# A fused image and text layer on one core: eight transfers of the rows of maxima, and another order within a turn

## The chip, the cores and the metric

One core of a Trainium2 chip runs the whole program. Its engines are TensorE (PE, matmuls and transposes), VectorE (DVE), ScalarE (ACT), GpSimd (POOL) and SyncE (SP, which issues most of the transfers). The metric is the device time of one execution in microseconds; lower is better.

## What is computed

The reference takes 32 images of 224 x 224 and 32 texts of 77 tokens. It embeds 196 patches per image with one matmul, adds positions, appends the texts (274 tokens of 192 numbers), and runs one layer: causal attention with 12 heads, then a two-sided mixture of experts with capacity.

```python
h = _L0_tok_ref(x, ...)                       # patches @ W.T + b, class token, positions
h = jnp.concatenate([h, txt], axis=1)         # (32, 274, 192)
h = h + _L0_attn_ref(_layernorm(h), ...)
h = h + _L0_ffn_ref(_layernorm(h), ...)

def _L0_attn_ref(X, Wq, bq, Wk, bk, Wv, bv, Wo, bo):
    q = rope(X @ Wq + bq)
    k = rope(X @ Wk + bk)
    v = X @ Wv + bv
    scores = jnp.einsum('bqhd,bkhd->bhqk', qh, kh) / jnp.sqrt(jnp.float32(hd))
    weights = jax.nn.softmax(jnp.where(causal, scores, -jnp.inf), axis=-1)
    out = jnp.einsum('bhqk,bkhd->bqhd', weights, vh).reshape(B, S, D)
    return out @ Wo + bo
```

## The kernel before

The program has two phases. The first, in the function `attention`, embeds, attends and routes, image by image; it fills about the first 1,000 us. The second, `experts`, runs the expert matmuls. The change touches the first alone.

**Tiling.** An image's 274 tokens are two tiles of 128 and a tail of 18. The tails of four images share one tile (`xnt`, `Vt`, `UsbT` and so on), so their work comes once in four images. The 12 heads are three groups (j = 0, 1, 2) of four.

**Turns.** Every engine runs the same loop, `for t in map(Turn, range(TURNS))`. In a turn five images are worked on at once, each in a later stage: `t.new` is embedded (E0 and E1, its two token tiles, lines 525, 1236 and 1252), `t.pre` is turned (X: transposes of its normed tokens `xn`, line 534), projected (V0, V1, QK0, QK1, lines 541 and 542), rotated on DVE (lines 1103, 1104) and its heads turned (KQ0 to KQ2, line 574); `t.mid` gets the maxima of its scores; `t.at` gets its scores and weights; `t.fin` its values (PV1, PV2), their transposes (UT0, UT1), division, AT and the output projection WO (lines 549, 550). `t.end` is added up and stored. Where an item is none, its lines are left out. The tails' steps (`t.tail[k]`: XTt, QKt, Vt, KQt0, KQt1, UTt, ATt, WOt) stand in one turn out of four each.

**Maxima and scores.** The softmax needs each query's maximum before its exponentials. Scores are computed twice. Round M*j* (`maxs`, line 587) writes the scores of a head group with queries on the partitions; `reduce_max` on DVE masks them into `capped` (line 1037) and reduces them along the keys into `nm` (lines 1039, 1041; the banks are free after the instruction of line 1039). A further round T (`maxs_tail`, lines 597 and 601) does this for the 18 tail queries, reduced at line 1299. PE transposes `nm` (MT, line 737), ACT rounds it into `mT[:, 0]` (line 852), DVE puts what is left over into `mT[:, 1]` (line 1325), and SP carries the rows of `mT` as further rows into `HX`, the operand of the score matmuls (lines 476, 477). In the next turn, round S*j* (`scores`, line 616) computes the scores again with keys on the partitions and the maximum taken off by these rows; ACT takes the exponential (`weights`, line 778), GpSimd masks (lines 911, 912), and PE multiplies with the values (PV*j*, `values`, line 628).

**Banks.** All rounds M, S and T share one set of four PSUM banks, `round_banks`, in the order M0, S0, M1, S1, M2, T, S2 of the table ROUNDS. A round starts when the one before it has been read (`fill_round`). All other results of PE (E0, X, V0 and so on) go to four further banks in turn, in the order of the table STEADY: each use waits until the use four places before it has been emptied, and the two tables must name the uses in the order in which PE's code issues them.

**Queues.** Every engine runs its instructions in the order in which the code issues them, and SP its transfers too. What can stall it is a semaphore. At the round S0 PE waits for all transfers of the rows of maxima:

```python
if j == 0:
    pe.wait_ge(mrow_in[b % 2], 224 * (b // 2 + 1))
```

PE's order in a turn before is: PV1, M0 (after a wait for KQ0, KQ1 and KQ2), PV2, E0, S0, X, E1, M1, V0, QK0, S1, UT0, UT1, QK1, (KQt), M2, V1, PV0, (XTt, ATt, UTt), T, AT, (RK, QKt), KQ0, KQ1, MT, S2, (Vt), KQ2, WO, (WOt).

## Time and profile before

| | us |
|---|---|
| median of 3 runs | 1520.82 |
| lowest and highest of them | 1489.72, 1523.75 |
| the profiled execution | 1509.2 |
| its span, first to last instruction | 1507.4 |
| mean granted TensorE clock over the span | 0.888 of full |
| PE busy | 1216.2 (81%) |
| DVE busy | 965.3 (64%) |
| ACT busy | 561.2 (37%) |
| POOL busy | 664.4 (44%) |

The rows below come from one profiled execution. A timeline row is start, duration, engine, line, operation, output<-inputs, and in brackets how long the engine had been idle and which instruction released it by the profile; neighbouring instructions of one kind are merged (x12). The brackets name what came last by the profile, not always the semaphore that held. SPq rows are issues of transfers. Overlapping instructions count once in busy times. Granted clock 1.00 is TensorE at 2.4 GHz, 0.5 at 1.2 GHz.

### The profile page before, as it was taken

The page shows a single profiled execution, that of the slowest core. Times are in us where ns is not written, and L with a number is a line of the kernel's source. Part 1 is how long each engine was busy: PE and PEld are TensorE (multiplying, and loading weights), DVE is VectorE, ACT ScalarE, POOL GpSimd, SP SyncE. Part 2 cuts the span into 40 slices and gives each one's busy share as a digit, 9 for nine tenths or more (in the row PEclk, how much of TensorE's full clock was granted, in tenths as well). Part 3 has the DMA queues.
Part 4 walks back from the last instruction along what each step waited for, and adds up shares of the span by engine and source line. Part 5 has one row for each costly group of instructions (what it writes and reads, how often), then busy time and mean ns, then how long its engine had stood idle before and what let it go on. Part 6 is the DMA issues. An engine that isn't in the chain of part 4 may idle for free.

```text
span 1507.4 us, 33177 instructions
## 1 busy us (share of the span) xinstructions
PE 1216.2 (81%) x12302; PEld 1013.1 (67%) x12302; DVE 965.3 (64%) x2211; ACT 561.2 (37%) x1039; POOL 664.4 (44%) x1097
## 2 busy tenths in 40 slices
PE   6688888888888888888888887763899687889993
PEld 5566666666666666665766665553799587889993
DVE  4657767778777776777778767646697433445441
ACT  1134434433433333333333433222355244445550
POOL 2134334334444543543454443342542665555665
PEclk8689989999999988989999987675899798999997
DMA  6011121113213212311231221138576565667751
GB/s 195 2 37 37 36 67 41 37 50 101 71 49 103 83 49 62 114 58 51 72 109 54 70 91 36 52 96 314 197 242 232 155 209 178 217 202 247 235 190 32
DMA packets 86676, 168.65 MB, mean 112 GB/s; under 512 B 17886, under 2 KB 60005, under 8 KB 86512
## 3 DMA queue, kind: packets, MB, share of 16 engines
q1 hardware_dynamic: 72848, 140.48, 29.3%
q0 software_dynamic: 13664, 26.00, 4.8%
q8 instruction: 101, 1.65, 0.5%
q14 instruction: 63, 0.52, 0.1%
HBM read 124.00 MB, written 45.45 MB: 112 GB/s over the span
## 4 chain that ended last, share of the span: by engine, by line
PE 37%; DVE 28%; issue 14%; SPq 9%; DMA 3%; POOL 3%; another core or an unknown queue 3%; ACT 2%; POOLq 0%; DVEq 0%; ACTq 0%
PE h_ps L1770 9%; PE y_ps L1781 7%; SPq L476 7%; PE gen L525 5%; DVE capped L1037 5%; DVE xn L1070 3%; DVE nm L1039 2%; PE round_banks L616 2%; DMA HX<-mT 2%; DVE ropeB L1104 2%; DVE ropeA L1103 2%; PE gen L534 2%; PE round_banks L601 1%; PE gen L628 1%
## 5 line engine op out<-in xcount | busy, mean ns | idle before, releaser
L778 ACT ACTIVATE PT<-round_banks 128x1752 f32<-128x1752 f32 x96 | 156.7, 1632 | 211.9 <-PE round_banks L616 210.9
L911 POOL TENSOR_SCALAR_AFFINE_SELECT PT<-PT 128x512 f32<-128x512 f32 x192 | 117.8, 638 | 210.8 <-ACT PT L778 210.4
L1860 ACT ACTIVATE Gl<-h_ps,W 128x256 f32<-128x256 f32 x264 | 117.4, 474 | 229.8 <-PE h_ps L1770 152.5
L1781 PE MATMUL y_ps<-W,Gl 128*128 128x192 f32 x1056 | 186.5, 329 | 7.3 <-issue 5.2
L1770 PE MATMUL h_ps<-XH,Wh 128*128 128x256 f32 x528 | 157.0, 312 | 43.0 <-issue 17.4
L1781 PEld LDWEIGHTS y_ps<-W,Gl 128*128 128x128 f32 x1056 | 174.1, 192 | 8.9 <-issue 6.9
L525 PE MATMUL gen<-w_emb,xT 128*128 128x192 f32 (+1 forms) x768 | 166.8, 377 | 7.9 <-DMA ident<-in_ident_dram 7.9
L525 PEld LDWEIGHTS gen<-w_emb,xT 128*128 128x128 f32 (+1 forms) x768 | 136.4, 193 | 22.1 <-DMA ident<-in_ident_dram 7.9
L1770 PE MATMUL h_ps<-XH,Wl 128*128 128x256 f32 x528 | 148.0, 299 | 0.0
L616 PEld LDWEIGHTS round_banks<-HX 18*128 18x128 f32 (+5 forms) x2304 | 79.4, 196 | 95.0 <-DMA HX<-mT 60.8
L1770 PEld LDWEIGHTS h_ps<-XH,Wh 128*128 128x128 f32 x528 | 110.2, 209 | 48.7 <-issue 34.9
L1670 POOL DMA_INDIRECT out_dram<-Y,sid x76 | 82.2, 1082 | 136.8 <-DVE Y L1953 117.6
L1037 DVE TENSOR_TENSOR capped<-round_banks,masks_f 128x1024 f32<-128x1024 f32 x96 | 116.3, 1212 | 37.0 <-PE round_banks L587 37.0
L616 PE MATMUL round_banks<-HX 18*128 18x146 f32 (+9 forms) x2304 | 88.2, 284 | 62.7 <-DMA HX<-mT 54.3
L1929 DVE TENSOR_TENSOR Wl<-W,Wh 128x768 fp32r<-128x768 f32 x88 | 84.2, 958 | 71.9 <-ACT Wh L1840 37.1
L1041 DVE TENSOR_REDUCE nm<-capped 128x8 f32<-128x1024 f32 x96 | 116.0, 1209 | 0.0
L1770 PEld LDWEIGHTS h_ps<-XH,Wl 128*128 128x128 f32 x528 | 110.3, 209 | 0.0
L1045 DVE SCALAR_TENSOR_TENSOR HX<-HX,slots,gen 128x512 fp32r<-128x512 f32 x96 | 70.0, 746 | 62.4 <-ACT HX L792 54.1
L628 PE MATMUL gen<-PT,V 128*17 128x274 f32 (+1 forms) x1536 | 97.1, 376 | 0.8 <-POOL PT L912 0.8
L920 POOL TENSOR_TENSOR rr<-ropeA,ropeB 128x384 f32<-128x384 f32 x64 | 65.9, 1030 | 70.5 <-DVE ropeB L1104 70.4
L541 PE MATMUL gen<-w_qkv,xnT 97*128 97x200 f32 (+1 forms) x256 | 92.7, 444 | 0.0
L587 PEld LDWEIGHTS round_banks<-HX 32*128 32x128 f32 (+1 forms) x1536 | 58.2, 203 | 50.8 <-issue 34.2
(276 smaller groups left out, 2508.3 us busy)
## 6 DMA issues: line engine op xcount, KB each, us to landing
W<-in_experts_dram SPq DMA_DIRECT2D x44, 771.0 KB
W<-in_experts_dram SPq DMA_DIRECT2D x44, 672.0 KB
xT<-in_xT_dram SPq DMA_DIRECT2D x32, 591.0 KB, 5.2
X<-sorted_d SPq DMA_DIRECT2D x35, 386.0 KB
stage<-rows_d SPq DMA_DIRECT2D x64, 192.0 KB
HX<-mT SPq DMA_DIRECT2D x384, 2.0 KB
rows_d<-h SPq DMA_DIRECT2D x32, 192.0 KB
out_dram<-h SPq DMA_DIRECT2D x32, 192.0 KB
```

The lines of the kernel that those rows point to most:

```text
L476: sp.dma_start(q[:, j, tok(k)], m[12 * j + 2 * k:12 * j + 12:3, :]).then_inc(mrow_in[b % 2], 16)
L525: mm = pe.matmul(g[0:m, 0:D], xT[b % 2][:, c, cols], w_emb[:, c, :], start=(c == 0), stop=(c == EC - 1))
L541: pe.matmul(o, xTs[:, 0, tok(k)], w[0:KC + 1, 0, cols], start=True, stop=False)
L616: mm = pe.matmul(R[0:m, i, at:at + n], x[rows, JG + j, klo:klo + m], q[rows, j, qlo:qlo + n], start=first, stop=not first, skip_group_chec ...
L628: mm = pe.matmul(g[SLOT * i:SLOT * i + HD + 1, lo:S], v, pt[:, i, at:at + n], start=(k == 0), stop=(k == 2), tile_position=(0, SLOT * i), ...
L778: act.activation(PT[(JG * b + j) % 2][:], R[:, :, 0:438], ACT.Exp, scale=SCALE).then_inc(exps, 1)
L911: pool.affine_select(x[:, :, at:at + P], x[:, :, at:at + P], [[0, GH], [1, P]], ALU.is_ge, 0.0, base=0, channel_multiplier=-1)
L1037: dve.tensor_tensor(capped[:], blocks[:, :, 0:3:2, :], masks[:].rearrange("p (a b k) -> p a b k", a=1, b=1).broadcast_to([P, GH, 2, P]), A ...
L1041: dve.tensor_reduce(x[:, :, 0:3:2], capped[:], AX.X, ALU.max, negate=True).then_inc(capped_read, 1)
L1770: mm = pe.matmul(h_ps[f % 3][:, 0:ROWS], w[t.par][:, cols], x, start=(k == 0), stop=(k == len(products) - 1))
L1781: mm = pe.matmul(y_ps[t.par][:, k * D:(k + 1) * D], Gl[t.par][:, f, k * P:(k + 1) * P], W[t.i][:, W2O + f * D:W2O + (f + 1) * D], start=(f ...
L1860: act.activation(Gl[t.par][:, f, :], h_ps[f % 3][:, 0:ROWS], ACT.Gelu, bias=W[t.i][:, B1O + f:B1O + f + 1]).then_inc(g_ready, 1)
```

## The change

Three things are changed, all within a turn.

1. **Rows of maxima.** `nm` has its columns by head (12) and tail (4) for each of the two token tiles, and the middle block's maxima go to a tile of their own, `nm1`. PE transposes it in two pieces to 16 rows of 256. A head group is then four neighbouring rows, and SP carries it with one transfer for each of the two parts of `mT`: eight transfers in all, the four of group 0 and of the tails first. Each head group has its own semaphore, and S*j* waits for its own rows.
2. **PE's order.** M0 comes first in the turn and no longer waits for KQ2 (M1 does). Then PV1, PV2, X, S0, E0, M1, V0, V1, QK0, S1, UT0, UT1, QK1, (KQt), M2, E1, (XTt, ATt, UTt), T, PV0, AT and on as before. The turned tokens X come ahead of S0, the first round with weights, and E1 ahead of T.
3. **The others follow.** On ACT the copy of X comes ahead of the exponential of S0, V1's copies behind V0's, and PV0's behind the tails' copies. On DVE E0's addition and first statistic stand just ahead of the second reduction, E1's addition, statistic and both aggregations behind the third, and the scaling of `xn` behind the remainder `mT`. On GpSimd the root for it stands behind the tail copy.

```diff
-STEADY = [("PV1", 4), ("PV2", 4), ("E0", 0), ("X", 1), ("E1", 0), ("V0", 1), ("QK0", 1), ("UT0", 4), ("UT1", 4), ("QK1", 1),
-          ("KQt0", "1"), ("KQt1", "1"), ("V1", 1), ("PV0", 3), ("XTt", "0"), ("ATt", "8"), ("UTt", "7"),
+STEADY = [("PV1", 4), ("PV2", 4), ("X", 1), ("E0", 0), ("V0", 1), ("V1", 1), ("QK0", 1), ("UT0", 4), ("UT1", 4), ("QK1", 1),
+          ("KQt0", "1"), ("KQt1", "1"), ("E1", 0), ("XTt", "0"), ("ATt", "8"), ("UTt", "7"), ("PV0", 3),
...
-        nm = sb("nm", [P, P])
-        mT = sb("mT", [P, 2, P], F32R)
+        nm = sb("nm", [P, 2, HEADS + GH])
+        nm1 = sb("nm1", [P, HEADS])
+        mT = sb("mT", [HEADS + GH, 2, 2 * P], F32R)
...
-                        for j in range(JG):
-                            for k in range(2):
-                                sp.dma_start(q[:, j, tok(k)], m[12 * j + 2 * k:12 * j + 12:3, :]).then_inc(mrow_in[b % 2], 16)
+                        sp.dma_start(q[:, 0, 0:2 * P], m[0:GH, :]).then_inc(mrow_in[0][b % 2], 16)
                         sp.dma_start(q[:, 0:JG, 2 * P:S],
-                                     m[36:40, 0:JG * SLOT].rearrange("i (j r) -> i j r", r=SLOT)[:, :, 0:TL]).then_inc(mrow_in[b % 2], 16)
+                                     m[HEADS:, 0:JG * SLOT].rearrange("i (j r) -> i j r", r=SLOT)[:, :, 0:TL]).then_inc(mrow_in[0][b % 2], 16)
+                    for j in range(1, JG):
+                        for w in range(2):
+                            q, m = HX[b % 3][HD + w:P:SLOT, 1].bitcast(F32), mT[:, w, :].bitcast(F32)
+                            sp.dma_start(q[:, j, 0:2 * P], m[GH * j:GH * j + GH, :]).then_inc(mrow_in[j][b % 2], 16)
...
-                if j == 0:
-                    pe.wait_ge(mrow_in[b % 2], 224 * (b // 2 + 1))
+                pe.wait_ge(mrow_in[j][b % 2], (64 if j == 0 else 32) * (b // 2 + 1))
...
+                if t.mid is not None:
+                    have("KQ0", t.mid)
+                    have("KQ1", t.mid)
+                    maxs(t.mid, 0)
                 if t.fin is not None:
                     values(t.fin, 1)
-                if t.mid is not None:
-                    for c in range(3):
-                        have(f"KQ{c}", t.mid)
-                    maxs(t.mid, 0)
...
-                    filled("MT", t.mid, pe.transpose(g[:, 0:P], nm[:], ident[:]))
+                    for k in range(2):
+                        mm = pe.transpose(g[0:HEADS + GH, tok(k)], nm[:, k, :], ident[:])
+                    filled("MT", t.mid, mm)
...
-                    act.activation(mT[:, 0, :], g[:, 0:P], ACT.Copy).then_inc(m_rounded, 1)
+                    act.activation(mT[:, 0, :], g[0:HEADS + GH, 0:2 * P], ACT.Copy).then_inc(m_rounded, 1)
```

The moved pieces read best as the engines' orders. First PE, a turn of kind B from the end of WO to the first rows of the projections (L587 is a round M, L616 a round S, L628 PV, L525 with 128 rows E0 and with 69 rows E1, L534 X), before:

```order
L587 MATMUL round_banks<-HX 128x256 x8
L587 MATMUL round_banks<-HX 128x128 x8
L628 MATMUL gen<-PT,V 17x274 x4
L628 MATMUL gen<-PT,V 17x146 x4
L628 MATMUL gen<-PT,Vt_2 17x18 x4
L525 MATMUL gen<-w_emb,xT 128x192 x6
L616 MATMUL round_banks<-HX 128x274 x8
L616 MATMUL round_banks<-HX 128x146 x8
L616 MATMUL round_banks<-HX 128x18 x8
L534 MATMUL gen<-ident,xn 96x128 x4
L525 MATMUL gen<-w_emb,xT 69x192 x6
L587 MATMUL round_banks<-HX 128x256 x8
```

and now, from the second of the two PV of that place on (every line number is higher by 2 or 3):

```order
L630 MATMUL gen<-PT,V 17x274 x4
L630 MATMUL gen<-PT,V 17x146 x4
L630 MATMUL gen<-PT,Vt_2 17x18 x4
L537 MATMUL gen<-ident,xn 96x128 x4
L618 MATMUL round_banks<-HX 128x274 x8
L618 MATMUL round_banks<-HX 128x146 x8
L618 MATMUL round_banks<-HX 128x18 x8
L528 MATMUL gen<-w_emb,xT 128x192 x6
L590 MATMUL round_banks<-HX 128x256 x8
L590 MATMUL round_banks<-HX 128x128 x8
```

X has moved from behind S0 to ahead of it, E0 from ahead to behind, and E1 is gone from between S0 and the next round M. The same rounds' places on DVE, from the last reduction of the turn, before (L1299 reduces T, L1325 is the remainder `mT`, the first L1103 and L1104 rotate QKt, which only kind A has):

```order
L1041 TENSOR_REDUCE nm<-capped 128x4x2
L1299 TENSOR_REDUCE nm<-round_banks 96x4
L1304 TENSOR_TENSOR nm<-nm 128x12
L1045 SCALAR_TENSOR_TENSOR HX<-HX,slots,gen 128x2x256 x2
L1325 TENSOR_TENSOR mT<-gen,mT 128x128
L1103 TENSOR_TENSOR ropeAt<-gen,cosw 128x384
L1104 TENSOR_TENSOR ropeBt<-gen,sinw 128x384
L1045 SCALAR_TENSOR_TENSOR HX<-HX,slots,gen 128x2x256
```

and now:

```order
L1046 TENSOR_REDUCE nm<-capped 128x4x2
L1280 TENSOR_TENSOR h<-gen,base 69x192
L1066 BN_STATS stat<-h 128x6
L1071 BN_AGGR mv<-stat 128x2 x2
L1296 TENSOR_REDUCE nm<-round_banks 96x4
L1300 TENSOR_TENSOR nm<-nm 128x12
L1050 SCALAR_TENSOR_TENSOR HX<-HX,slots,gen 128x2x256 x2
L1321 TENSOR_TENSOR mT<-gen,mT 16x256
L1075 TENSOR_SCALAR xn<-h,mv,rstd 128x192 x2
L1108 TENSOR_TENSOR ropeAt<-gen,cosw 128x384
L1109 TENSOR_TENSOR ropeBt<-gen,sinw 128x384
L1050 SCALAR_TENSOR_TENSOR HX<-HX,slots,gen 128x2x256
```

E1's addition, statistic and aggregations stand between the third reduction and that of T, and the scaling of `xn` between the remainder and the rotation of QKt. SP's transfers of a turn, before and now:

```order
L476 DMA HX<-mT 4x128 x6
L477 DMA HX<-mT 4x3x18
L476 DMA HX<-mT 4x128 x6
L477 DMA HX<-mT 4x3x18
L392 DMA xT<-in_xT_dram 128x1182
```

```order
L475 DMA HX<-mT 4x256
L476 DMA HX<-mT 4x3x18
L475 DMA HX<-mT 4x256
L476 DMA HX<-mT 4x3x18
L481 DMA HX<-mT 4x256 x4
L393 DMA xT<-in_xT_dram 128x1182
```

Fourteen issues became eight, and the four that S0 waits for are the first.

## Rows read from the trace of the kernel before

**Rows 1.** Busy time by stretch (length, engines, PEclk, DMA share, GB/s): turns, then many

```profile
238.80:269.90 31.10, 26.87 (x312) 21.42 (x310) 23.13 (x51) 13.39 (x28) 12.22 (x24) 0.89 0.16 48
269.90:296.50 26.60, 21.59 (x295) 16.60 (x295) 20.22 (x42) 9.93 (x17) 9.94 (x20) 1.00 0.17 51
296.50:323.90 27.40, 21.90 (x299) 16.75 (x299) 21.08 (x46) 10.97 (x21) 9.93 (x20) 1.00 0.16 48
323.90:354.00 30.10, 26.70 (x307) 19.89 (x308) 24.11 (x62) 10.08 (x18) 10.93 (x23) 0.89 0.21 63
...
528.00:558.20 30.20, 24.91 (x299) 18.91 (x299) 21.05 (x46) 10.97 (x21) 13.41 (x25) 0.89 0.19 60
...
238.80:916.60 677.80, 568.42 (x6949) 436.13 (x6947) 509.63 (x1153) 256.22 (x464) 299.97 (x574) 0.92 0.23 70
```

**Rows 2.** Groups by line, PE: busy, mean ns | idle before, by releaser

```profile
L616 PE MATMUL round_banks<-HX 18*128 18x146 f32 (+9 forms) x2304 | 88.2, 284 | 62.7 <-DMA HX<-mT 54.3 <-DVE nm L1039 6.4 <-ACT PT L778 1.7
```

**Rows 3.** Timeline of kind B, first part: start, us, engine, line, tiles [idle before]

```profile
271.32 0.28 DVE L1325 TENSOR_TENSOR mT<-gen,mT 128x128 fp32r<-128x128 f32 x1
...
271.64 3.25 SPq L476 DMA_DIRECT2D HX<-mT  x6
...
273.47 0.75 DVE L1045 SCALAR_TENSOR_TENSOR HX<-HX,slots,gen 128x512 fp32r<-128x512 f32 x1 [1.86 <-ACT HX L792]
...
274.47 0.69 PE L587 MATMUL round_banks<-HX 32*128 32x256 f32 x16 [0.63 <-ACT Usb L782]
...
275.20 1.23 DVE L1037 TENSOR_TENSOR capped<-round_banks,masks_f 128x1024 f32<-128x1024 f32 x1 [0.44 <-PE round_banks L587]
...
275.97 2.22 PE L525 MATMUL gen<-w_emb,xT 128*128 128x192 f32 x12
...
276.35 0.68 DVE L1039 TENSOR_REDUCE nm<-round_banks 128x4 f32<-128x512 f32 x1
...
278.83 0.57 SPq L477 DMA_DIRECT2D HX<-mT  x1
...
280.44 0.66 DVE L1070 TENSOR_SCALAR xn<-h,mv,rstd 128x192 f32<-128x192 f32 x2
...
280.49 0.88 PE L616 MATMUL round_banks<-HX 32*128 32x274 f32 x24 [2.31 <-DMA HX<-mT]
...
281.42 1.63 ACT L778 ACTIVATE PT<-round_banks 128x1752 f32<-128x1752 f32 x1 [4.89 <-PE round_banks L616]
```

**Rows 4.** Timeline of the same turn, second part

```profile
283.93 0.35 DVE L1252 TENSOR_TENSOR h<-gen,base 69x192 f32<-69x192 f32 x1 [2.83 <-PE gen L525]
...
284.20 0.60 DVE L1061 BATCH_NORM_STATS2 stat<-h 128x6 f32<-128x192 f32 x2
...
285.01 1.19 DVE L1037 TENSOR_TENSOR capped<-round_banks,masks_f 128x1024 f32<-128x1024 f32 x1
...
288.77 1.35 DVE L1070 TENSOR_SCALAR xn<-h,mv,rstd 128x192 f32<-128x192 f32 x2
...
288.93 1.07 POOL L920 TENSOR_TENSOR rr<-ropeA,ropeB 128x384 f32<-128x384 f32 x1 [2.40 <-DVE ropeB L1104]
...
292.03 1.22 DVE L1037 TENSOR_TENSOR capped<-round_banks,masks_f 128x1024 f32<-128x1024 f32 x1
...
293.99 0.32 PE L597 MATMUL round_banks<-tmask,identb 128*96 128x18 bf16 x4 [1.78 <-DVE nm L1039]
...
295.09 1.30 DVE L1299 TENSOR_REDUCE nm<-round_banks 96x4 f32<-96x1096 f32 x1
...
296.52 0.33 PE L737 MATMUL gen<-ident,nm 128*128 128x128 f32 x1
```

**Rows 5.** Timeline of kind A, the projection of the tails' values (Vt)

```profile
241.98 1.04 PE L541 MATMUL gen<-w_qkv,xntT 97*128 97x200 f32 x2 [2.10 <-DVE ropeBt L1104]
```

**Rows 6.** Timeline, S0 of the last two turns

```profile
929.31 1.39 PE L616 MATMUL round_banks<-HX 32*128 32x274 f32 x24 [4.03 <-DMA HX<-mT]
...
962.92 1.49 PE L616 MATMUL round_banks<-HX 32*128 32x274 f32 x24 [4.91 <-DMA HX<-mT]
```

More of the change, by code:

```diff
@@ L349, in attention @@
         nmax_ready = sem("nmax_ready")
-        mrow_in = sems("mrow_in", 2)
+        mrow_in = [sems(f"mrow{j}_in", 2) for j in range(JG)]
         exps, masked = sem("exps"), sem("masked")
@@ L669, in _ @@
                     turn_tokens("X", t.pre, xn, 2)
+                if t.at is not None:
+                    scores(t.at, 0)
                 if t.new is not None:
-                    embed(t.new, 1)
+                    embed(t.new, 0)
                 if t.mid is not None:
+                    have("KQ2", t.mid)
                     maxs(t.mid, 1)
@@ L965, in _ @@
                     pool.tensor_copy(HX[b % 3][:, :, :, 2 * P:S], HXt[:, :, :, b % 4, :].bitcast(F32)).then_inc(tails_copied, 1)
+                if t.new is not None:
+                    root(LN1, t.new, 2)
+                    root_std(t.new)
                 if t.tail[0] is not None:
```

94 lines of the change are left out of this document (44 added, 50 removed).

## The prediction

> **What bounds the kernel now.** I first cut the span into turns by their TensorE (PE) transposes of `nm`, and put the busy times of the turns side by side [rows 1]. A turn has one image in each of five stages, and four kinds of turn repeat, since the tails of four images share a tile. I call them A (from 238.8 us), B (269.9), C (296.5) and D (323.9). In B, PE is busy 21.6 of 26.6 us and VectorE (DVE) 20.2, so neither fills it: the turn is a chain between them through the one set of round banks. The reader should see there that PE computes a round of scores, DVE or ScalarE reads it, and only then can PE write the next. Next came the groups by line, for what PE waits for: 54.3 us before the first score round S0, for the rows of maxima that SP copies into `HX` [rows 2]. The timeline of B shows both halves of it. `mT` is ready at 271.6, 14 transfers follow at 0.54 each, the last is issued at 278.83, and S0 starts at 280.49, 1.66 us after that issue; PE stood for 2.31 us [rows 3]. Everything behind S0 is late with it: ScalarE's exp (1.63), then E1, then DVE, which stands 2.83 us until E1 is there, and only then the second max reduction at 285.01 [rows 3, 4].
>
> **The change, part by part.** I take B from `mT` ready to the next `nm` transpose.
>
> *Rows of maxima.* S0 now waits for four transfers, not fourteen: 0.54 + 0.57 + 0.54 + 0.57 = 2.2 us of issue, the last beginning at 271.6 + 1.65 = 273.3; plus 1.66 they are there at 275.0, where they were at 280.4. A row transfer is now twice as long (4 rows of 256 numbers). The trace has no such transfer; below, it costs what one of 128 costs (0.54), above, as much as the two it replaces (1.08), which puts the landing at 276.1. I take the first. The four for j = 1 and 2 begin before 276 and are wanted 6 us later at the earliest. PE makes two transposes of `nm` for one (0.3 us more), ScalarE and DVE copy 256 columns for 128 (0.28 each now [rows 3]; at most twice that, 0.3 more each).
>
> *M0 first, without KQ2.* The 0.63 us before M0 carries the name of a ScalarE copy, but M0 starts right after DVE's `HX` piece of KQ2 ends (273.47 + 0.75 = 274.22) and the code has the wait for KQ2 there [rows 3]. It goes to M1. But DVE has KQ2's piece and two additions ahead of the reduction anyway: its 0.44 us of idleness before 275.20 say that it was done at 274.8, and there the reduction now begins. The banks are free after the second of its three instructions (1.23 + 0.68), at 276.8. PE has M0, PV1 and PV2 until E0's old start less the 0.63, 275.3, then X (half a us), and waits about 1 us. S0 runs at 276.8 instead of 280.49: 3.7 earlier, and the rows (275.0) leave 1.8 to spare. If that cover is gone, each us of later landing costs one.
>
> *E0 after S0, E1 behind M2.* exp ends at 276.8 + 0.93 + 1.63 = 279.4, E0 (2.2) at 279.9, so M1 loses 0.5 to E0. DVE must finish `xn2`, which hangs on GpSimd and not on S0 (280.44 + 0.66 = 281.1), then E0's addition and one statistic (0.65): the second reduction starts at 281.8 instead of 285.01, 3.2 earlier. From there to the third reduction it took 7.0 [rows 4]; of these, 1.35 was scaling `xn`, which goes behind `mT`: 5.75, so the third is at 287.5 instead of 292.03, 4.5 earlier. E1 on PE fills the 1.78 us in which PE stood before the tail round T. What pays is DVE: its block for E1 took 285.01 - 283.93 = 1.1, of which one statistic (half of 0.60) has gone ahead with E0; 0.8 now stands between the third reduction and that of T, where nothing hides it. The next `nm` transpose is thus 4.5 - 0.8 = 3.7 earlier, at 292.8. PE's own side: T starts 1.96 behind the third reduction, at 289.5; from T to that transpose it took 2.53, and PV0 comes on top (0.9, as PV2 between M0's end at 275.16 and E0 at 275.97): 292.9, just as late. For hops between engines and for this tightness I take off 1.0: **B saves 2.7 us, C the same**. GpSimd's root for `xn` moves behind its tail copy; behind it stand the tail addition and the last causal mask, which come later than it anyway: nothing.
>
> *`xn` behind `mT`.* Its two instructions take 1.35 us where GpSimd's addition of `rr` (1.07) runs beside them, and 0.66 for the same shape (`xn2`) elsewhere [rows 3, 4]. In B and C DVE waits 1.86 us for ScalarE's KQ2 copy just there, which hides it. The Trainium skill (SBUF — State Buffer, Who interferes with whom) says that VectorE and GpSimd share a port pair as an exclusive lock, and the second to come blocks wholly. The two rows agree with it; by the rule the moved pair costs 0.66 where GpSimd is idle and up to a GpSimd instruction more where not.
>
> *Kind A pays.* Its Vt projection waits 2.10 us for DVE's rotation of QKt [rows 5], and `xn` now stands ahead of that rotation: 0.7 to 1.35 more. A has no wait before S0 to win. DVE's later `xn` slot is free, but ScalarE's tail copies end late there, so that gain is mostly lost, and E1's 0.8 comes at the end. Bounds: +0.3 and +2.3; I take **A +1.3**. *Kind D* waited little before S0, but wins the order from M0 to M1 and `xn`'s slot (1.35), and loses 0.8: between 0.5 and 3; I take **-2.0**.
>
> *Sum.* Four turns: -2.7 - 2.7 + 1.3 - 2.0 = -6.1. From the second turn to the last are 30, or 7.5 fours: -46. The last two turns wait 4.03 and 4.91 before S0 [rows 6], more than the 2.3 counted: -5. Then the clock: 238.8 to 916.6 had a mean granted clock of 0.92 [rows 1], that is, stretches at 1.2 of 2.4 GHz that lose up to 0.08 x 678 = 54 us. A and D at 0.89 lose 3.4 each, 39 in the 5.8 fours; 15 are left to B and C, 19 over all 7.5. The same kind C took 27.4 at 1.00 and 30.2 at 0.89. With gaps of about 1 us in place of 2.3 most of that should go: -14. Altogether -65. The profiled execution took 1509.2 (span 1507.4), so 1444; the median of the three runs is 11.6 above it, so **1456 us** there.
>
> **The rivals.**
>
> *Only half is kept.* The gaps move to bank release, E0 delays M1 more than I laid out, or ScalarE's later Usb and `attT` copies hold KQ0. For it: PE and DVE meet within 0.1 us at the end of B in my layout. Against: the second reduction really waited on E1, which waited on S0. B and C save 1.4, D 1, A pays 1.3: -2.5 x 7.5 = -19, ends -5, clock -7: -31, 1490 by the median.
>
> *Nothing is kept.* The rows' wait is hidden slack of a DVE-bound turn and the change moves where PE idles. Against it speak 2.83 us of DVE idleness right behind that wait. About 1515.
>
> *Slower: the end of the turn on DVE.* One mechanism: E1's 0.8 ahead of T's reduction and `xn` (up to 1.35) ahead of the QKt rotation lengthen the path from the third reduction to the next M0 in every turn, while the second reduction does not come earlier. It decides if in B that reduction starts less than 0.8 us earlier than 285.01. Price: 0.8 x 30 = 24, A's rotation 1.35 x 7.5 = 10: +34, 1555.
>
> *The clock stays up.* Gaps of 1 us may leave PE at 2.4 GHz in D too and shorten A's stretch: of the 54 us, 45 come back instead of 14. -46 - 5 - 45 = -96, 1425. Against: A's gap grows to about 3 us and D's behind S2 stays. The Trainium skill (TensorE: Matmul & The Clock Gate, HAM oscillation — how this bites in real kernels) has PE fall to half clock after an idle stretch and stay there until it has been busy a while. The trace agrees only in part: B took a 2.31 us gap at clock 1.00.
>
> **How the numbers follow.** Forecast 0.60 (1436 to 1478 around 1456); half kept 0.16; nothing kept 0.08; slower 0.06; clock stays up 0.10. The range 1425 to 1495 holds the forecast, most of the half and of the clock case, about 8 in 10; the three runs of before spread by 34 us, which this must also cover. A measurement here tells about 2% (30 us) from no change, so faster means below 1490: all of the forecast and of the clock case, and half of the half case, 0.78. Within 2%: the other half and nothing kept, 0.16. Slower: 0.06.
>
> **What would show it.** In the profile after: no idle time before S0 put down to `HX<-mT` beyond a few us in total; S0 about 4 us after M0 in B, with DVE's release before it; DVE no longer idle at E1's addition; PE idle before T under 1 us; A turns longer than 31 us with over 2.5 us before Vt; B and C near 24 us at clock 1.0. I would be wrong if B's second reduction keeps its distance of 9.8 us from the first, if the rows land after 276.8, or if the share of low clock rises.

## The result, and the profile after

| us | before | after |
|---|---|---|
| median of four runs | 1512.12 | 1411.69 |
| lowest and highest | 1489.72, 1523.75 | 1405.82, 1436.51 |
| ratio, with its 95% interval | | 0.9398 [0.9269, 0.9528] |
| the profiled execution, its span | 1509.2, 1507.4 | 1415.52, 1413.7 |
| mean granted clock over the span | 0.888 | 0.911 |
| the 28 turns A to D, seven times | 827.8 | 748.4 |
| granted clock in these | 0.91 | 0.95 |

The change makes the kernel 6.0% faster by the ratio. (The quotient of the two medians is 0.934, inside the interval of the ratio.) An execution now and then comes out some per cent slower than the others of its kernel, whatever the kernel, and the ratios are formed without these. The direction and the main mechanism were forecast; the size was not. The profiled execution is 93.7 us shorter, the forecast was 65, and the median lies below the range that I gave.

First the turns again, by stretch (length, busy time of PE, PE's weight loads, DVE, ACT and POOL, granted clock, DMA share and GB/s), in the kernel after: B, C, D and A as in [rows 1], a later D and A, and the 28 turns.

```profile
245.00:268.30 23.30, 21.41 (x296) 16.53 (x296) 20.39 (x42) 10.00 (x17) 9.64 (x20) 1.00 0.20 58
268.30:293.00 24.70, 21.66 (x301) 16.80 (x301) 21.78 (x48) 10.83 (x19) 10.03 (x21) 1.00 0.18 54
293.00:320.60 27.60, 23.33 (x310) 17.99 (x308) 24.54 (x62) 10.80 (x19) 11.01 (x23) 1.00 0.24 69
320.60:349.60 29.00, 25.04 (x312) 20.11 (x310) 23.20 (x55) 13.60 (x28) 15.96 (x29) 0.94 0.29 92
...
398.20:428.10 29.90, 26.43 (x311) 20.87 (x309) 25.06 (x62) 10.84 (x19) 11.08 (x23) 0.89 0.22 64
428.10:460.10 32.00, 28.05 (x312) 22.03 (x309) 23.44 (x55) 13.54 (x28) 15.81 (x29) 0.84 0.26 83
...
107.60:856.00 748.40, 657.02 (x8456) 511.65 (x8455) 625.93 (x1378) 316.03 (x559) 350.85 (x676) 0.95 0.24 73
```

The same 28 turns of the kernel before:

```profile
122.70:950.50 827.80, 693.16 (x8427) 530.50 (x8425) 613.28 (x1371) 310.34 (x559) 351.18 (x676) 0.91 0.22 66
```

B and C now run at full clock each time, and are 3.3 and 2.7 shorter than the B and C of [rows 1], which had clock 1.00 as well. D ran at 0.89 in [rows 1]; here one D has 1.00 and another 0.89. A is on average as long as it was, 29 to 32, and its length goes with its granted clock.

Then the groups that waited. PE before the rounds S and DVE before the reduction, after (busy, mean ns | idle before them, by releaser; before in [rows 2]):

```profile
L618 PE MATMUL round_banks<-HX 18*128 18x146 f32 (+9 forms) x2304 | 83.8, 273 | 48.5 <-DVE nm L1044 44.4 <-DMA HX<-mT 1.9 <-ACT PT L782 1.8
L600 PE MATMUL round_banks<-tmask,identb 128*96 128x18 bf16 x128 | 10.3, 189 | 12.3 <-DVE nm L1044 12.2
```

```profile
L1042 DVE TENSOR_TENSOR capped<-round_banks,masks_f 128x1024 f32<-128x1024 f32 x96 | 116.7, 1215 | 5.7 <-PE round_banks L590 5.7
```

The wait for the transfers fell from 54.3 to 1.9 over the whole phase. A shorter one for DVE's release of the banks stands there, 48.5 in all before 96 rounds. DVE hardly waits for a round M any more, 5.7 us in 96 reductions where it was 37.0.

The timeline of the first B (start, us, engine, line, tiles, and in brackets the idle time before and its releaser), to be laid beside [rows 3, 4]:

```profile
246.37 0.41 DVE L1321 TENSOR_TENSOR mT<-gen,mT 16x256 fp32r<-16x256 f32 x1
246.81 0.53 SPq L475 DMA_DIRECT2D HX<-mT  x1
...
248.10 0.69 PE L590 MATMUL round_banks<-HX 32*128 32x256 f32 x16
248.57 0.57 SPq L476 DMA_DIRECT2D HX<-mT  x1
249.19 2.15 SPq L481 DMA_DIRECT2D HX<-mT  x4
249.88 1.22 DVE L1042 TENSOR_TENSOR capped<-round_banks,masks_f 128x1024 f32<-128x1024 f32 x1
251.84 0.88 PE L618 MATMUL round_banks<-HX 32*128 32x274 f32 x24 [0.84 <-DVE nm L1044]
...
254.70 1.23 POOL L915 TENSOR_SCALAR_AFFINE_SELECT PT<-PT 128x512 f32<-128x512 f32 x2
254.83 1.11 DVE L1093 SCALAR_TENSOR_TENSOR by_token<-by_token,rstd,w_r 128x8 f32<-128x8 f32 x2 [1.20 <-issue]
...
257.11 1.21 DVE L1042 TENSOR_TENSOR capped<-round_banks,masks_f 128x1024 f32<-128x1024 f32 x1
262.59 2.17 PE L528 MATMUL gen<-w_emb,xT 128*69 128x192 f32 x12
263.09 1.22 DVE L1042 TENSOR_TENSOR capped<-round_banks,masks_f 128x1024 f32<-128x1024 f32 x1
265.05 0.32 PE L600 MATMUL round_banks<-tmask,identb 128*96 128x18 bf16 x4 [0.29 <-DVE nm L1044]
265.94 0.34 DVE L1280 TENSOR_TENSOR h<-gen,base 69x192 f32<-69x192 f32 x1
266.95 1.26 DVE L1296 TENSOR_REDUCE nm<-round_banks 96x4 f32<-96x1096 f32 x1
268.34 0.39 PE L740 MATMUL gen<-ident,nm 128*16 128x128 f32 x2
```

The reader should see the chain in its new order. A transfer of 256 costs 0.53, the row that was not in the trace of before. S0 starts 3.74 after M0, released by DVE; it was 6.02 (280.49 - 274.47 in [rows 3]). From the first to the second reduction it is 7.23 where it was 9.81, and E1 (262.59) fills the stretch ahead of T, where PE now stands for 0.29.

### The profile page after: what moved, and what is told of

Its sections match the earlier page's. It is cut to its first block and busy times, and to the rows that moved or that the text cites. A ratio compares the mean times of both kernels' runs of the same rounds, so it can differ in the third digit from the quotient of the medians.

```text
span 1413.7 us, 33145 instructions
## 1 busy us (share of the span) xinstructions
PE 1169.9 (83%) x12334; PEld 986.8 (70%) x12334; DVE 974.2 (69%) x2211; ACT 567.6 (40%) x1039; POOL 662.6 (47%) x1097
## 5 line engine op out<-in xcount | busy, mean ns | idle before, releaser
L528 PE MATMUL gen<-w_emb,xT 128*128 128x192 f32 (+1 forms) x768 | 150.9, 350 | 8.1 <-DMA ident<-in_ident_dram 8.1
L1774 PEld LDWEIGHTS h_ps<-XH,Wh 128*128 128x128 f32 x528 | 109.0, 206 | 61.4 <-issue 47.7
L528 PEld LDWEIGHTS gen<-w_emb,xT 128*128 128x128 f32 (+1 forms) x768 | 123.2, 178 | 17.8 <-DMA ident<-in_ident_dram 8.1
L618 PEld LDWEIGHTS round_banks<-HX 18*128 18x128 f32 (+5 forms) x2304 | 76.1, 185 | 79.5 <-issue 75.0
L786 ACT ACTIVATE Usb<-gen 128x274 f32<-128x274 f32 x96 | 38.5, 401 | 219.8 <-PE gen L630 217.2
L618 PE MATMUL round_banks<-HX 18*128 18x146 f32 (+9 forms) x2304 | 83.8, 273 | 48.5 <-DVE nm L1044 44.4
L924 POOL TENSOR_TENSOR rr<-ropeA,ropeB 128x384 f32<-128x384 f32 x64 | 63.8, 997 | 126.9 <-DVE ropeB L1109 126.9
L237 POOL DMA_INDIRECT sorted_d<-stage,pos x72 | 73.5, 1020 | 36.8 <-DMA stage<-rows_d 20.1
```

The lines of the kernel that those rows point to most:

```text
L528: mm = pe.matmul(g[0:m, 0:D], xT[b % 2][:, c, cols], w_emb[:, c, :], start=(c == 0), stop=(c == EC - 1))
L618: mm = pe.matmul(R[0:m, i, at:at + n], x[rows, JG + j, klo:klo + m], q[rows, j, qlo:qlo + n], start=first, stop=not first, skip_group_chec ...
L1774: mm = pe.matmul(h_ps[f % 3][:, 0:ROWS], w[t.par][:, cols], x, start=(k == 0), stop=(k == len(products) - 1))
```

## The experiments

Ratios are to the kernel before, run on the same chip, with their 95% intervals. "28 turns" is that stretch of the profiled execution each time, from the third `nm` transpose to the 31st: 827.8 us at clock 0.91 before, 748.4 at 0.95 after. Edits are shown as diffs against the kernel before or after, as named, with parts left out at "...".

The experiments were run in three groups on three chips. The kernel before had a median of 1490.69 us beside the first group (the parts apart, E1 back, rotation first), 1519.15 beside the second (22 and 20 fillings, M0 back, the choice behind `xn`) and 1510.64 beside the third (9 and 8 fillings, the choice in the next turn, `xn` back). So the 28 turns and the clocks of two kernels, and two ratios from different groups, should be compared with some reserve. A turn at clock 1.00 is a better measure: B took 23.6 to 23.7 us in most turns of all the kernels with B's order as in after, whatever the chip.

### The parts apart: the transfers alone, the order alone

Transfers alone is the kernel before with `nm`, `nm1`, `mT`, the eight transfers and a semaphore for each group; no engine's order changes but for these.

```diff
# against before
-                        for j in range(JG):
-                            for k in range(2):
-                                sp.dma_start(q[:, j, tok(k)], m[12 * j + 2 * k:12 * j + 12:3, :]).then_inc(mrow_in[b % 2], 16)
+                        sp.dma_start(q[:, 0, 0:2 * P], m[0:GH, :]).then_inc(mrow_in[0][b % 2], 16)
...
```

> The kernel before with only the rows of maxima changed: eight transfers, a semaphore for each head group, the new layout of nm. Order of every engine as before. Theory 1 (the two parts need each other: short transfers take away the wait before S0, the order turns it into earlier reductions): S0 in kinds B and C comes 2.3 us earlier, right behind E0, DVE's idle time before E1's addition shrinks from 2.8 to about 0.5; B and C save 2.3 each, 35 us over the program, the last two turns 5 to 9, and with the gaps before S0 gone the clock gives back 10 to 20: ratio to before 0.955 to 0.97. Theory 2 (the order alone does it, the transfers had slack to lose): ratio 0.99 or more. Theory 3 (the transfers alone do it): ratio near 0.94, as the whole change.

Measured: 0.9587 [0.9492, 0.9683]; 28 turns 767.0 at 0.94. PE's wait before the rounds S was 13.5 us, none of it for transfers. The stretches that the new order is for are still there (the three groups as above):

```profile
L618 PE MATMUL round_banks<-HX 18*128 18x146 f32 (+9 forms) x2304 | 84.5, 275 | 13.5 <-DVE nm L1045 11.7 <-issue 1.8
L600 PE MATMUL round_banks<-tmask,identb 128*96 128x18 bf16 x128 | 10.7, 193 | 42.9 <-DVE nm L1045 42.9
L1043 DVE TENSOR_TENSOR capped<-round_banks,masks_f 128x1024 f32<-128x1024 f32 x96 | 116.3, 1212 | 28.6 <-PE round_banks L590 28.6
```

At clock 1.00 its B took 24.3 us, its C 24.8 to 25.2 and its D 27.9. Against the lengths of before at full clock (26.6, 27.4 and 30.3; the last one comes from a run below) the transfers alone win 2.3, 2.5 and 2.4.

Order alone is the kernel after with fourteen transfers of 128 and S0 waiting for all of them.

```diff
# against after
-                        sp.dma_start(q[:, 0, 0:2 * P], m[0:GH, :]).then_inc(mrow_in[0][b % 2], 16)
+                        for j in range(JG):
+                            for k in range(2):
+                                sp.dma_start(q[:, j, tok(k)], m[GH * j:GH * j + GH, tok(k)]).then_inc(mrow_in[0][b % 2], 16)
...
-                pe.wait_ge(mrow_in[j][b % 2], (64 if j == 0 else 32) * (b // 2 + 1))
+                if j == 0:
+                    pe.wait_ge(mrow_in[0][b % 2], 224 * (b // 2 + 1))
```

> The kernel after with the rows carried by fourteen transfers again, each 4 rows of 128 numbers, and S0 waiting for all of them; all else as after. Theory 1: the last transfer lands about 8.9 us after mT is ready, S0 would be due about 5.2 us after it, so B, C and D wait 3 to 4 us before S0 with everything behind it late: 25 us or more of the gain per 100 us are lost again, ratio to before 0.97 to 1.00, idle time before S0 of 80 us and more put down to the transfers. Theory 2 (order alone): ratio 0.95 or less and little idle time before S0.

Measured: 1.0207 [1.0093, 1.0321]. The interval lies above 1, a loss, where neither theory had one. 28 turns took 840.5 at 0.89, and PE stood before S for

```profile
L617 PE MATMUL round_banks<-HX 18*128 18x146 f32 (+9 forms) x2304 | 96.8, 303 | 129.1 <-DMA HX<-mT 125.4 <-DVE nm L1042 1.9 <-ACT PT L781 1.7
```

The 54.3 of [rows 2] became 125.4. E0 (2.22 us), which covered part of the landing ahead of S0, now stands behind it, and only X (0.64) takes its place. The parts are worth -4.1% and +2.1% apart and -6.0% together: without early rows the order costs time. How much it adds once the rows land early is less certain. The ratios of the transfers alone and of both overlap a little (0.9492 to 0.9683 and 0.9269 to 0.9528). At full clock the order takes another 0.6 us off B, some 0.3 off C and 0.3 off D.

### E1's place, and then `xn`'s

E1 back behind E0, on PE and on DVE, all else as after. The second experiment also puts the scaling of `xn` back ahead of the attention's rotations.

```diff
# against after
-STEADY = [("PV1", 4), ("PV2", 4), ("X", 1), ("E0", 0), ("V0", 1), ...
+STEADY = [("PV1", 4), ("PV2", 4), ("X", 1), ("E0", 0), ("E1", 0), ("V0", 1), ...
...
                     embed(t.new, 0)
+                    embed(t.new, 1)
...
```

> The kernel after with E1 and its work on DVE back behind E0, ahead of M1 and of the second reduction; xn stays behind mT, all else as after. Theory (the late E1 is what lets the second reduction start early): M1 comes 2.1 us later, so does the second reduction, and PE stands about 1.8 us before T again; DVE gets 0.8 back at the end of the turn. B, C and D lose 1.3 to 2 us each: 30 to 40 us, ratio to before 0.96 to 0.97. Rival (DVE is the bound at the turn's end, E1's place on PE does not matter): the 0.8 is won in every turn and the time falls by up to 20 us, ratio 0.925 to 0.935.

> The kernel with E1 back behind E0 (ratio to before 0.987) and xn back between the rotation of QK0 and the divisions, GpSimd's root with it. Theory (xn's old slot beside GpSimd's addition costs DVE 1.27 to 1.35 between the second and the third reduction, its new one 0.64): 0.7 to 1.3 us in B, C and D, 10 to 30 us on top, less 0.6 in A: ratio 0.99 to 1.01. Rival (with E1 early PE stands 1.9 to 2.9 us before T anyway and DVE's chain is not the bound): 0.98 to 0.99, as without.

Measured: 0.987 [0.9789, 0.995] and 0.9798 [0.9734, 0.9862]. With E1 behind E0 some four fifths of the gain go, which is more than I expected, and the kernel is slower than with the transfers alone (0.9587). From the first of the two, a group by line, a turn of kind D and the 28 turns:

```profile
L600 PE MATMUL round_banks<-tmask,identb 128*96 128x18 bf16 x128 | 12.1, 204 | 72.4 <-DVE nm L1043 72.4
...
199.48:233.20 33.72, 29.08 (x307) 21.88 (x304) 21.50 (x44) 11.11 (x20) 10.85 (x23) 0.80 0.13 39
...
118.50:930.10 811.60, 693.95 (x8456) 538.90 (x8454) 628.39 (x1378) 317.31 (x559) 348.26 (x676) 0.89 0.22 67
```

The wait before T is 72.4 in place of 12.3 (2.4 in each B, 2.9 in each A), and the clock over the 28 turns is 0.89 in place of 0.95. M1 stands behind both halves of the embedding there. At full clock B took 24.5 and C 25.0, 0.9 and 0.4 more than after; the rest of the loss is in A (32.4 on average), in D (31.5) and in the clock. Putting `xn` back as well made no further loss that the ratios show (their intervals overlap). At full clock it made B 24.9 and C 25.3, 0.4 and 0.3 more, where I had given it 1.35 us a turn in D and part of the third reduction's 4.5.

### M0's place

M0 back behind PV1, with its wait for KQ2.

```diff
# against after
+                if t.fin is not None:
+                    values(t.fin, 1)
                 if t.mid is not None:
-                    have("KQ0", t.mid)
-                    have("KQ1", t.mid)
+                    for c in range(3):
+                        have(f"KQ{c}", t.mid)
                     maxs(t.mid, 0)
                 if t.fin is not None:
-                    values(t.fin, 1)
...
```

> The kernel after with M0 behind PV1 again and with the wait for KQ2 ahead of M0 instead of M1; all else as after. The layout of the prediction had DVE free for the first reduction 0.4 us before M0 in B and C. Theory: 0.4 to 0.7 us in B and C and up to 1.5 in A and D, where M0 comes at a low clock: 10 to 25 us of the gain are lost, ratio to before 0.946 to 0.957. Rival (M0's place is worth nothing, DVE sets the first reduction anyway): 0.94.

Measured: median 1429.02 (1404.62 to 1434.41) beside 1519.15 for before. No ratio is on record for it. In its profile, at clock 1.00 each time, B and C took 0.5 us more than after, and PE stood 0.63 before M0. That is the size expected of it in B and C, but it is not shown beyond that trace.

### What holds A, and the clock

In A the gap before Vt had grown from 2.10 [rows 5] to 2.68. Is A long because `xn` stands ahead of the rotation of QKt (0.6 us), or because of what that does to the clock? The rotation was put first:

```diff
# against after, on DVE: behind the remainder mT
+                if t.tail[0] is not None:
+                    g = t.tail[0]
+                    if g:
+                        dve.wait_ge(rrt_ready, g)
+                    rotate("QKt", g, 2, ropeAt[:], ropeBt[:])
                 if t.new is not None:
                     b = t.new
...
                     scale(LN1, 0, xn[:, 0, :], h[b % 8][:, 0, :])
                     scale(LN1, 1, xn[:, 1, :], h[b % 8][:, 1, :]).then_inc(xn_ready, 1)
...
-                if t.tail[0] is not None:
...
-                    rotate("QKt", g, 2, ropeAt[:], ropeBt[:])
```

> The kernel after with DVE's rotation of QKt ahead of the scaling of xn; only kind A (one turn in four) has it. The gap before Vt shrinks from 2.68 to about 2.05 us. Theory A (the gap costs its length alone): 0.6 x 8 = 5 us less, ratio to before about 0.937. Theory B (this gap is what lets TensorE's clock fall in A, which then runs 3 to 10 us at the lower level): with 2.05 the stretches of low clock in A get shorter or rarer, A's 32 us turns become 29 or less and up to 15 us are won, ratio about 0.93. Before the change the gap was 2.1 to 2.2 and A still had 0.89, which speaks for A.

Measured: 0.9296 [0.9206, 0.9385]. This interval overlaps that of after (0.9269 to 0.9528), so the gain over it rests on the trace. The gap went back to 2.11, 0.57 less, and A to 28.1 on average from 30.5, 2.4 less. Kinds B, C and D stayed within 0.15 us. At full clock this A takes 27.5, 0.6 less than after by the estimate further down, so 0.6 of the 2.4 is the gap and 1.8 the clock. An A at clock 0.94, one at 1.00, and the 28 turns of this kernel:

```profile
317.47:345.88 28.41, 25.09 (x312) 20.09 (x309) 23.77 (x55) 13.46 (x28) 15.86 (x29) 0.94 0.29 94
...
424.50:452.00 27.50, 23.50 (x312) 18.55 (x310) 23.70 (x55) 13.58 (x28) 15.91 (x29) 1.00 0.30 97
...
108.70:841.10 732.40, 643.94 (x8456) 502.83 (x8455) 630.01 (x1378) 315.55 (x559) 351.13 (x676) 0.97 0.24 74
```

Two more fill that gap rather than shorten it: matmuls of `ident` by 64 of its columns, whose result nobody reads, into the bank that the next use overwrites. The output is unchanged. The first has 22 of them in the kernel after, the second 8 in the kernel with the rotation first.

```diff
# against after; the second also has the rotation first, and 8 for 22
                 if t.tail[0] is not None:
+                    if t.pre is not None:
+                        keep_busy(22, "KQ2", t.pre)
                     project("Vt", t.tail[0], xntT, w_qkv, 0, slice(2 * D, 3 * D + NE))
```

> The kernel after with 22 matmuls of no use (128 x 64, into KQ2's free bank) on TensorE in kind A, between S2 and the projection Vt, where it otherwise stands 2.68 us. Theory A (that gap lets the clock fall in A): A runs at 1.00, about 27.3 us instead of 29 to 32, 2 to 5 us in each of 7 turns, ratio to before 0.92 to 0.93. Theory B (A's low clock has another cause, or the filling delays what follows): 0.935 to 0.945.

> QKt's rotation ahead of xn, and 8 matmuls of no use (1.9 us) in the gap of 2.1 before Vt in kind A. The run with 22 fillings took 5 us in a gap of 2.7, so its A turns were 30.4 each time, 2.3 of it excess. Theory (the clock falls in A for this gap): A at 1.00 and 26.8 to 27.3 us in every turn, against 27.5 to 28.4 without the filling: 5 to 10 us, ratio to before 0.92 to 0.925. Rival: A as without the filling, ratio 0.93.

Measured: 0.9292 [0.9197, 0.9387] and 0.9197 [0.9123, 0.927]. The 22 fillings last about 5 us in a gap of 2.7, and A is still not longer (30.5 on average, as after, but at clock 1.00 each time); what they add in time the clock gives back. Its 28 turns took 749.5, as after. The 8 fit, A took 27.5 to 27.8, and one of them reads

```profile
312.50:340.00 27.50, 25.48 (x329) 20.45 (x327) 23.72 (x55) 13.56 (x29) 16.02 (x29) 1.00 0.30 98
```

This is the lowest ratio of the study. Its interval just meets that of after, and overlaps that of the rotation alone, so the filling by itself is not shown to gain over the rotation.

### The clock's share, measured alone

The kernel before, with fillings ahead of the wait of S0 in B and C and nothing moved.

```diff
# against before
                 if t.at is not None:
+                    if t.t % 4 in (2, 3) and t.pre is not None:
+                        keep_busy(9, "X", t.pre)
                     scores(t.at, 0)
```

> The kernel before with 20 matmuls of no use (128 x 64, into X's free bank) on TensorE just ahead of S0's wait, in the turns of kinds B and C alone; the results and all waits are as before. They fill about 2 of the 2.3 us for which TensorE stands there. Theory A (that gap is what lets the clock fall in B and C): B and C run at granted clock 1.00 every time, 26.6 and 27.4 us instead of 27.8 and 29.1 on average: 15 to 25 us less although nothing else moved, ratio to before 0.983 to 0.99. Theory B (the clock falls for other gaps, in A and D, and by chance of timing): no turn gets shorter, ratio 1.00 or a little over, where the filling lasts longer than the wait.

> The kernel before with 9 matmuls of no use ahead of S0's wait in kinds B and C (18 instructions, since each took two in the run with 20, at 0.115 us: 2.1 us, no more than the wait; the 20 had taken 4.6). With 20, every turn B took 28.7 and C 29.2 us at clock 1.00, about 2.3 of it the filling's excess. Theory A (the 2.3 us gap is what lets the clock fall): B 26.6 to 26.8 and C 27.2 to 27.4 in every turn, 20 us less in all, ratio to before 0.98 to 0.99. Theory B (the excess of the filling only hid a fall that comes by chance): B and C go on varying by 2 to 3 us, ratio 1.00.

Measured: with 20 of them 1.0016 [0.9972, 1.006], with 9 of them 0.9893 [0.9841, 0.9945]. Each filling shows as two instructions of 0.115 us, so 20 took 4.6 us in a gap of 2.3 and delayed S0 by about 2. B and C ran at 1.00 but for the first of each, and took 28.8 and 29.3 on average, where they were 27.8 and 29.1. Nine took 2.1 and fit. Then S0 starts no later, the transfers land no earlier, and the program is still 1.1% faster, 15 us between the medians. The trace of one B and of the 28 turns:

```profile
271.48 2.12 PE L609 MATMUL gen<-ident 128*128 128x64 f32 x18
273.95 0.89 PE L622 MATMUL round_banks<-HX 32*128 32x274 f32 x24 [0.36 <-DMA HX<-mT]
...
121.70:924.90 803.20, 695.35 (x8680) 541.55 (x8677) 613.33 (x1371) 311.68 (x559) 351.52 (x676) 0.94 0.22 68
```

803.2 at 0.94 in place of 827.8 at 0.91: on average A is 28.9 where it was 30.4, C 27.6 where it was 29.1, B and D hardly shorter (27.4 and 30.8). Kind A has no filling and the same gap before Vt, 2.10, yet four of its seven turns ran at 1.00 in 28.2 to 28.4 us, and none did so in the profile of before. So the clock of a turn seems to hang on the gaps of the turns ahead of it too. That is read from two profiles of different groups of runs, and not shown further.

These two runs also show what A and D of the kernel before take at full clock, which its own trace has nowhere: an A of the run with 9, and a D of the run with 20, which has no filling in it, with its S0.

```profile
350.50:378.70 28.20, 23.79 (x311) 18.54 (x309) 23.45 (x55) 13.29 (x28) 16.05 (x29) 1.00 0.30 94
...
690.20:720.50 30.30, 23.72 (x307) 18.02 (x308) 24.21 (x63) 10.12 (x18) 10.95 (x23) 1.00 0.22 63
...
703.13 0.83 PE L622 MATMUL round_banks<-HX 32*128 32x274 f32 x24 [2.31 <-DMA HX<-mT]
```

That D waits 2.31 for the rows of maxima, as much as B.

### What holds D

In D of the kernel after PE stands 1.03 before WO, 0.78 before X and 1.66 before S0. DVE's routing choice for the tails (`choose`) stands there. I moved it behind `xn`, and then into the next turn.

```diff
# against the kernel with the rotation first; the second puts it behind the LN2 aggregate of the next turn
-                if t.tail[11] is not None:
+                if t.tail[11] is not None and t.hurried:
                     choose(t.tail[11])
...
                     scale(LN1, 1, xn[:, 1, :], h[b % 8][:, 1, :]).then_inc(xn_ready, 1)
+                if t.tail[11] is not None and not t.hurried:
+                    choose(t.tail[11])
```

> The kernel with the rotation of QKt ahead of xn, and DVE's choice of experts (11 small instructions, 2.4 us, kind D) moved from ahead of KQ0's and KQ1's pieces to behind mT and xn. In D WO no longer waits for KQ0 (1.04), mT and xn are ready 2.4 earlier, and the choice falls into the time in which DVE waits for ScalarE's copy of KQ2; S0's wait for the first reduction (1.67) shrinks if DVE was late for it. Theory: D saves 1 to 2.5 us and its clock stays at 1.00: 10 to 20 us, ratio to before 0.915 to 0.925. Rival (the choice then delays KQ2's piece, WO's addition and the first reduction by as much): no gain, 0.93.

> QKt's rotation ahead of xn, and DVE's choice of experts in the next turn, behind the statistics of the second norm, where DVE waits 0.7 to 1.0 us for GpSimd's root. It no longer stands ahead of KQ0's and KQ1's pieces, as in after, nor ahead of KQ2's, as in the run with the late choice, where X then waited 2.84. Theory: in D the waits before WO (1.04), X (0.77) and S0 (1.67) shrink to under 1.5 together, the second reduction of D comes 1.4 later for the choice; D saves 1 to 2 us and stays at clock 1.00: 8 to 20 us, ratio to before 0.915 to 0.925. Rival (DVE is the bound in D wherever the choice stands): 0.93.

Measured: 0.9276 [0.9162, 0.9389] and 0.9249 [0.9191, 0.9308], beside 0.9296 [0.9206, 0.9385] without. Behind `xn` the choice delays DVE's piece of KQ2 and X waits 2.84 us for that bank; the wait moved. In the next turn the wait before WO goes, but 1.14 before X and 1.67 before S0 stay, and D took 28.4 in its profile, as without. Neither is told from no gain.

## Why the prediction was wrong in size

In short, three terms of the sum were too small. The four turns without the clock, booked at -6.1, came to -8.6, above all because A was charged 1.3 and paid nothing, and because D was taken to wait little for the transfers and had B's wait. The start of the program gave 12 us more than booked. The clock, booked at 14, gave some 19.

The profiled executions split the 93.7 us: 6.5 before the first `nm` transpose, 8.4 in turns 1 and 2, 79.4 in the 28 turns, 4.3 in the last turn, and 5.1 lost in the second phase, which the change does not touch. By kind, over the 28 turns (mean of seven, from `nm` transpose to `nm` transpose):

| us | A | B | C | D | four turns |
|---|---|---|---|---|---|
| before | 30.4 | 27.8 | 29.1 | 31.0 | 118.3 |
| after | 30.5 | 23.6 | 24.6 | 28.2 | 106.9 |
| rotation first | 28.1 | 23.6 | 24.6 | 28.3 | 104.6 |

These means mix what the change does at a given clock with what the clock does. To part them, here is what each kind takes at clock 1.00, in steady turns, beside what I forecast without the clock:

| us at full clock | A | B | C | D | four turns |
|---|---|---|---|---|---|
| before | 28.2 | 26.6 | 27.4 | 30.3 | 112.5 |
| after | 28.1 | 23.6 | 24.6 | 27.6 | 103.9 |
| difference | -0.1 | -3.0 | -2.8 | -2.7 | -8.6 |
| forecast | +1.3 | -2.7 | -2.7 | -2.0 | -6.1 |

A and D of before are from the two runs with fillings, in turns that have none. A of after never ran at full clock; 28.1 is an estimate, the 27.5 of the kernel with the rotation first and 0.57 for its shorter gap, and the 22 fillings give the same (30.4 less the 2.3 by which they overrun).

**Rows landed at 275.0: right as far as the trace shows.** Transfers of 256 cost 0.53 to 0.54, the last of the four begins 2.2 behind the start of `mT`'s remainder (248.57 - 246.37) where 2.0 was forecast, and no S0 of the steady turns waits for one. The landing itself has no row.

**M0 first, S0 3.7 earlier: right.** In the new B, S0 comes 5.5 behind `mT` (251.84 - 246.37); it was 9.2 (280.49 - 271.32): 3.7 earlier.

**Second reduction 3.2 earlier: nearly.** 10.74 behind `mT` against 13.69 is 2.95. Part of what I left out is in the row of L1093 above: 1.11 beside a GpSimd mask, in DVE's way to this reduction, where the same two took 0.36 before.

**Third reduction 4.5, the turn 3.7 earlier, 1.0 taken off for hops: B and C -2.7 each: right.** At full clock they took 3.0 and 2.8 less. PE's wait before T is 0.29, under the 1 us named. The third reduction is 16.72 behind `mT` (it was 20.71), 4.0 earlier and not 4.5. Most of the step came with the transfers: alone they gave 2.3 in B and 2.5 in C. With all of the change but E1's place B had 24.5 and C 25.0, so that place is worth 0.9 and 0.4, and `xn`'s slot 0.4 and 0.3 on top of that.

**A +1.3: the first step that failed, by its balance.** The gap before Vt grew by 0.57, just under the 0.7 to 1.35 worked out, and with the rotation first it went back. But I booked no gain in A, and there was one: in the A of [rows 5] PE stood 1.17 before T, after 0.83; waits of 0.44 before `rrt` and 0.18 before S0 are gone. At full clock A is some 0.1 shorter, 1.4 off the forecast, and on average, with the clock, 0.2 longer.

**D -2.0: the second, wrong in its cause.** It came to -2.7 at full clock. I had it "waited little before S0" from the D of [rows 1], where PE waited 0.44. Here are two D of the kernel before with the same mean clock, 0.89, each cut where S0 starts, and their S0:

```profile
323.90:336.60 12.70, 10.76 (x113) 8.12 (x113) 9.45 (x27) 3.63 (x6) 2.69 (x8) 0.73 0.02 3
336.60:354.04 17.44, 15.98 (x194) 11.80 (x195) 14.71 (x36) 6.48 (x12) 8.24 (x16) 1.00 0.35 106
558.20:571.20 13.00, 9.26 (x113) 7.04 (x113) 9.80 (x29) 3.63 (x6) 3.61 (x9) 0.87 0.02 5
571.20:590.40 19.20, 17.68 (x195) 12.88 (x195) 14.44 (x34) 6.50 (x12) 7.34 (x14) 0.91 0.33 98
...
336.62 0.83 PE L616 MATMUL round_banks<-HX 32*128 32x274 f32 x24 [0.44 <-DMA HX<-mT]
...
571.28 0.83 PE L616 MATMUL round_banks<-HX 32*128 32x274 f32 x24 [2.30 <-DMA HX<-mT]
```

S0 starts 12.7 and 13.1 us into the turn whether the clock ahead of it was 0.73 or 0.87: the transfers set its time. In the first of these turns the low clock lay ahead of S0, stretched the work there and so filled the wait, at no cost; in the second the wait shows in full, 2.30, and low clock behind S0 makes the rest of the turn 19.2 long in place of 17.4. At full clock D had B's wait for the rows, and the transfers alone took 2.4 off it (27.9 at full clock). After, PE stands 1.03 before WO, 0.78 before X and 1.66 before S0, none of it for transfers, and its low clock falls behind S0, where it costs 2.3 (29.9 or 30.0 for 27.6).

**The sum of the four turns, -6.1: the term that was mis-sized most.** At full clock it is -8.6, and of the 2.5 missing 1.4 are A's and 0.7 D's. Over the 28 turns that is 60 us where I had 42.7, 17 more.

**The clock -14: too low, by less.** The four got 11.4 shorter, so 2.8 a four, some 19 us in the 28 turns, are left for the clock. By kind, the mean less the length at full clock was 2.2 in A, 1.2 in B, 1.7 in C and 0.7 in D, and is 2.4, 0, 0 and 0.6: B and C gave back all they had lost, 20 us, and A and D nothing, as I had it. The most that the low clock can have cost over the 28 turns is 0.09 x 828 = 75 us before and 0.05 x 748 = 37 after. What it did cost, by the table, was 41 and 21; the D above shows one place where low clock costs nothing, ahead of a wait that something else ends. The run with nine fillings does show A's clock rise with no edit in A (28.9 for 30.4), but in the kernel after A's clock did not rise.

The Trainium skill (TensorE: Matmul & The Clock Gate, A second HAM failure mode: psum-queue depth-cycling) describes a kernel whose short idles between groups of matmuls make the clock go up and down. The traces agree: in A and C, gaps of 2.1 to 2.8 us, with PE busy some 80% of the turn, are where the clock often fell, and filling them brought it back. They agree with the objection in my prediction as well, that one such gap need not bring it down: B took 2.31 at 1.00, and after, A takes 2.68 each time and is at 0.94 or 0.84.

**The ends: the start was put at nothing.** I let the 7.5 fours carry turns 1 and 2 at the mean, 3.1 for the two. They gave 8.4, and 6.5 came before the first `nm` transpose (64.5 to 57.9 us from the start), which I had not counted at all. It goes with E1's place: of the eight kernels with E1 late, seven have this transpose at 57.7 to 58.9 and one at 61.4; the six with E1 early have it at 61.5 to 64.5 (the transfers alone 63.8, E1 put back 63.8). The last turn gave 4.3 of the -5.

In all, in the profiled execution: the 28 turns gave 79.4 where 42.7 and 14 were forecast, 22.7 more, of which some 17 are the turns at full clock and 5 the clock. With 6.5 + 5.3 from the start, less 0.7 and less 5.1 of the second phase, that is the 29 us between 65 and 93.7. Two slips in the working, 5.75 for 7.0 - 1.35 and 0.9 for a PV2 of 0.81, are 0.1 each and change nothing.

**The signs.** Right: no wait for `HX<-mT` in steady turns, S0 about 4 us after M0 with DVE's release before it, DVE not idle at E1's addition, under 1 us before T, over 2.5 before Vt, B and C near 24 at clock 1.00; and none of the three signs of being wrong came. Wrong: A over 31 each time, it was so in three turns of seven.

**What the rivals were worth.** "The clock stays up" has the nearest number, 1425, but by luck: of its 45 us from the clock some 19 came, the low clock of A and D stayed, and what made up the difference were the turns at full clock and the start. "Only half is kept" (-2.5 a four) is far from -8.6. "Slower: the end of the turn on DVE" does not occur, since the second reduction came 2.95 earlier and it needs less than 0.8. "Nothing is kept" needs a DVE-bound turn; DVE is near it only now (5.7 us idle before 96 reductions).

What stays open: why D is at 1.00 in one four and at 0.89 in the next (and the A behind it at 0.94 and 0.84) with gaps of the same length; how much the choice in D is worth; and what the first and the last D, which differ in work from the others, take at full clock.

## What to carry over

Lay turns of one kind side by side at full clock before pricing anything. A mean clock does not say what the low clock costs, and the length of a wait in one turn does not say how long it is: here low clock ahead of D's S0 shrank its wait for the transfers from 2.3 to 0.4 us, and made a turn that had as much to win as B look like one that had little. Book gains in every kind of turn, not only in those that the change aims at, and in the start of the program. Filling a gap of known length with idle matmuls that fit into it prices the clock alone, with nothing moved (here 1.1%), and also brings turns to full clock that can then be read. A reordering that takes cover from a transfer and a shortening of that transfer should be judged together: here -4.1% and +2.1% apart were -6.0% as one.
